# The shared expert's last 64 hidden columns: gate and up in one stationary block, the product across partitions

## The reference, cut to what matters

```python
I_MOE, I_SH = (176, 704)
logits = h @ router_w.T                       # which four experts a token takes
...
g = jnp.einsum('nh,ehi->eni', h, w_gate)      # the routed experts
u = jnp.einsum('nh,ehi->eni', h, w_up)
y = jnp.einsum('eni,eih->enh', jax.nn.silu(g) * u, w_down)
routed = jnp.einsum('enh,ne->nh', y, comb)
shared = jax.nn.silu(h @ sh_gate) * (h @ sh_up) @ sh_down
sg = jax.nn.sigmoid(h @ sh_gate_w)
return (routed + sg * shared).reshape(orig)
```

## Time and profile before

| what | value |
|---|---|
| median of 3 runs | 572.34 us (570.43 to 573.94) |
| the profiled execution | 572.58 us |
| its span, first to last instruction | 570.7 us |
| TensorE busy | 494.5 us of the span |
| mean granted clock of TensorE | 0.951 of full speed |

### The profile page before, as it was taken

The page is one execution under the profiler, slowest core; times in us unless marked ns, Lnnn a source line. Parts: engine busy times, 40 slices in busy tenths (PEclk is TensorE's granted clock), DMA queues, the critical chain, the costliest instruction groups (busy, mean ns, idle before and its releaser), DMA issues.

```text
span 570.7 us, 11095 instructions
## 1 busy us (share of the span) xinstructions
PE 494.5 (87%) x3334; PEld 433.5 (76%) x3338; DVE 446.4 (78%) x1374; ACT 352.7 (62%) x909; POOL 331.7 (58%) x316
## 2 busy tenths in 40 slices
PE   0699989989799998995568999999999999589794
PEld 0477767877698997994358999999999998346582
DVE  4789967966879897855667888989899987859784
ACT  2344547343567675763228887888888889756543
POOL 2547671014368886416698899898777873451300
PEclk9999989999999999996587999999999999959998
DMA  8144454312364656545820000010000000000001
GB/s 279 38 120 138 133 156 121 89 55 65 106 201 113 192 159 202 145 134 148 277 65 29 18 22 28 21 29 1 3 1 2 2 1 2 0 1 0 20 18 38
DMA packets 27960, 45.24 MB, mean 79 GB/s; under 512 B 5696, under 2 KB 18848, under 8 KB 27264
## 3 DMA queue, kind: packets, MB, share of 16 engines
q1 hardware_dynamic: 21056, 28.15, 16.3%
q0 software_dynamic: 3792, 10.74, 7.4%
q10 hardware_dynamic: 3056, 5.65, 3.0%
HBM read 34.63 MB, written 8.85 MB: 76 GB/s over the span
## 4 chain that ended last, share of the span: by engine, by line
PE 49%; DVE 22%; POOL 10%; issue 9%; ACT 5%; DMA 4%; SPq 1%; ACTq 0%; DVEq 0%; POOLq 0%
PE bank L1111 8%; PE bank L432 7%; PE bank L433 7%; PE bank L434 7%; PE bank L1555 5%; POOL yk L629 2%; PE bank L1313 2%; PE bank L1315 2%; PE bank L1314 2%; POOL Q_lo L678 1%; PE bank L1508 1%; DVE X L1676 1%; POOL Q L672 1%; DMA seg<-seg_dram 1%; POOL pr L665 1%
## 5 line engine op out<-in xcount | busy, mean ns | idle before, releaser
L601 POOL DMA_INDIRECT inb<-rows_kept,row_of x47 | 47.1, 1002 | 35.4 <-PE bank L1111 19.3
L984 ACT ACTIVATE pr<-sc,smin 128x256 f32<-128x256 f32 x128 | 63.6, 505 | 0.0
L678 POOL TENSOR_TENSOR Q_lo<-Q,Q_hi 128x512 fp32r<-128x512 f32 x32 | 41.5, 1296 | 15.3 <-ACT Q_hi L729 14.3
L2135 DVE CUSTOM_DVE_ANT_0 sc<-bank,bias 128x256 f32<-128x256 f32 x128 | 46.6, 421 | 0.0
L1624 DVE TENSOR_TENSOR pT_lo<-bank,pT_hi 128x512 fp32r<-128x512 f32 x64 | 41.2, 684 | 6.8 <-ACT pT_hi L729 6.6
L729 ACT ACTIVATE pT_hi<-bank 128x512 fp32r<-128x512 f32 x64 | 35.0, 596 | 15.1 <-PE bank L1111 14.7
L559 POOL TENSOR_TENSOR Wd<-wd_raw,Wd 128x512 fp32r<-128x512 f32 x13 | 16.8, 1293 | 42.2 <-ACT Wd L776 42.2
L672 POOL TENSOR_TENSOR Q<-Q,rot 128x512 f32<-128x512 f32 x32 | 41.1, 1283 | 0.0
L665 POOL TENSOR_TENSOR pr<-pr,srec 128x512 f32<-128x512 f32 x32 | 33.3, 1042 | 13.3 <-DVE srec L2142 13.2
L432 PE MATMUL bank<-K_hi,Q_hi 128*128 128x256 f32 x128 | 37.2, 291 | 4.3 <-POOL Q_lo L678 4.3
L629 POOL DMA_INDIRECT yk<-slots_y,slot x32 | 32.9, 1027 | 10.8 <-issue 5.5
(11 more groups left out here) (351 smaller groups left out, 1954.1 us busy)
## 6 DMA issues: line engine op xcount, KB each, us to landing
slots_y<-yb SPq DMA_DIRECT2D x47, 128.0 KB
wg_raw<-gate_up_dram SPq DMA_DIRECT2D x22, 256.0 KB, 2.6
bw<-bits_dram ACTq DMA_DIRECT2D x3, 1024.0 KB
wd_raw<-down_dram SPq DMA_DIRECT2D x16, 128.0 KB, 2.2
wo<-wo_dram SPq DMA_DIRECT2D x2, 1024.0 KB, 5.7
wd_raw<-down_dram SPq DMA_DIRECT2D x30, 64.0 KB, 2.4
gu_raw<-gate_up_dram SPq DMA_DIRECT2D x6, 256.0 KB, 3.6
X<-x_dram SPq DMA_DIRECT2D x2, 512.0 KB, 6.7
```

Source lines behind the costliest of these rows:

```text
L601: pool.indirect_dma_start(inb[:, j % NIN, :], None, rows_d, bass.IndirectOffsetOnAxis(row_of[:, j:j + 1], 0)).then_inc(slots_in[j % NIN], 16)
L678: pool.tensor_tensor(Q_lo[:, i % 2, :], Q[:, i % 2, :], Q_hi[:, i % 2, :].bitcast(F32), ALU.subtract).then_inc(queries_low_g, 1)
L984: e = act.activation(pr[:, i % 2, z, :], sc[:, i % 2, z, :], ACT.Exp, bias=smin[:, i % 2, z:z + 1], scale=-1.0, accum_out=ssum[:, i % 2, z ...
L2135: dve.tensor_tensor_reduce(sc[:, r, z, :], bank[2 + h][:, u * S:(u + 1) * S], bias[:, TB * b_ + u, :], 1.0, 3.0e38, ALU.add, ALU.min, smin ...
```

## The change

Units 10 and 11 no longer compute with the zeros. The 64 gate columns and the 64 up columns of the last chunk are laid side by side in one block of 128 while the weights are split (gate_and_up reads them from gu_raw, gate_beside_up writes them), so six matmuls give both: the gate on partitions 0 to 63 of one bank, the up on partitions 64 to 127 of the same bank. silu, the product and the splits of hid work on 64 partitions; the product reads gsil from partitions 0 to 63 and the up from partitions 64 to 127. The down matmuls contract over 64 partitions. FULL is 10, the number of units on whole chunks, and HALF_CHUNK is 64. up_p, the count of finished up groups, ends at 10 now, so the last layer's use of that semaphore counts from FULL. No transfer changes; the number of instructions on ScalarE, VectorE, GpSimd and SyncE stays.

```diff
--- before.py
+++ after.py
@@ -410,6 +410,20 @@
         def shared_bank(v, g):
             return (2 * v + g) % 3
 
+        FULL = 2 * (I_SH // P)
+        HALF_CHUNK = I_SH % P
+
+        def rows_of(v):
+            return slice(0, P) if v < FULL else slice(0, HALF_CHUNK)
+
+        def gate_and_up(part, c):
+
+            return part[:, c % 2, :].rearrange("p (g k m) -> p k g m", g=2, k=KD)[:, :, :, 0:HALF_CHUNK]
+
+        def gate_beside_up(part, c):
+
+            return part[:, c % 2, 0:KD * P].rearrange("p (k g m) -> p k g m", g=2, k=KD)
+
         def dn_buffer(e):
 
             return e % 2 if e < NT else 2 if e < EARLY_E else e - EARLY_E
@@ -806,7 +820,11 @@
                 act.wait_ge(gate_up_in[c % 2], 16 * (c // 2 + 1))
                 if c >= 2:
                     act.wait_ge(up_p, 2 * (c - 1))
-                copy(gu_hi[:, c % 2, :], gu_raw[:, c % 2, :]).then_inc(gate_up_high_a, 1)
+                if 2 * c < FULL:
+                    ins = copy(gu_hi[:, c % 2, :], gu_raw[:, c % 2, :])
+                else:
+                    ins = copy(gate_beside_up(gu_hi, c), gate_and_up(gu_raw, c))
+                ins.then_inc(gate_up_high_a, 1)
 
             def hi_dn(c):
                 act.wait_ge(down_in[c % 2], 16 * (c // 2 + 1))
@@ -860,13 +878,15 @@
                 act.wait_ge(gate_p, v + 1)
                 if v >= 2:
                     act.wait_ge(hidden_v, v - 1)
-                act.activation(gsil[:, v % 2, :], bank[shared_bank(v, 0)][:, :], ACT.Silu).then_inc(gate_silu_a, 1)
+                rows = rows_of(v)
+                act.activation(gsil[rows, v % 2, :], bank[shared_bank(v, 0)][rows, :], ACT.Silu).then_inc(gate_silu_a, 1)
 
             def hi_hid(v):
                 act.wait_ge(hidden_v, v + 1)
                 if v >= 2:
                     act.wait_ge(down_p, v - 1)
-                copy(hid_hi[:, v % 2, :], hid[:, v % 2, :]).then_inc(hidden_high_a, 1)
+                rows = rows_of(v)
+                copy(hid_hi[rows, v % 2, :], hid[rows, v % 2, :]).then_inc(hidden_high_a, 1)
 
             def ternary_end(i, c):
                 act.wait_ge(ternary_v, 5 * i + 2 + c)
@@ -1206,7 +1226,7 @@
                     pe.wait_ge(prep_read_v, EARLY)
                     pe.wait_ge(x_after1_v, NE0 * NT)
                 cols = slice(n * HALF, (n + 1) * HALF)
-                for g in range(2):
+                for g in range(2 if v < FULL else 1):
                     if g == 0 and v >= 2:
                         pe.wait_ge(hidden_v, v - 1)
                     if g == 1 and v >= 1:
@@ -1251,8 +1271,9 @@
                     t = n * (NT // 2) + x
                     tile = slice(x * P, (x + 1) * P)
 
-                    e = split3(pe, bank[4 + t // 2][:, (t % 2) * D:(t % 2 + 1) * D], hid_hi[:, v % 2, tile],
-                               hid_lo[:, v % 2, tile], dn_hi[:, c % 2, :], dn_lo[:, c % 2, :],
+                    rows = rows_of(v)
+                    e = split3(pe, bank[4 + t // 2][:, (t % 2) * D:(t % 2 + 1) * D], hid_hi[rows, v % 2, tile],
+                               hid_lo[rows, v % 2, tile], dn_hi[rows, c % 2, :], dn_lo[rows, c % 2, :],
                                c == 0 and t % 2 == 0, c == C_SH - 1, skip_group_check=True)
                 e.then_inc(down_p, 1)
 
@@ -1760,7 +1781,11 @@
 
             def lo_gu(c):
                 dve.wait_ge(gate_up_high_a, c + 1)
-                lo(gu_lo[:, c % 2, :], gu_raw[:, c % 2, :], gu_hi[:, c % 2, :]).then_inc(gate_up_low_v, 1)
+                if 2 * c < FULL:
+                    ins = lo(gu_lo[:, c % 2, :], gu_raw[:, c % 2, :], gu_hi[:, c % 2, :])
+                else:
+                    ins = lo(gate_beside_up(gu_lo, c), gate_and_up(gu_raw, c), gate_beside_up(gu_hi, c))
+                ins.then_inc(gate_up_low_v, 1)
 
             def lo_dn(c):
                 dve.wait_ge(down_high_a, c + 1)
@@ -1918,19 +1943,22 @@
                 dve.tensor_scalar(row_of[:, :], row_f[:, :], N - 1.0, None, ALU.min).then_inc(routing_v, 1)
 
             def hidden(v):
-                dve.wait_ge(up_p, v + 1)
+                if v < FULL:
+                    dve.wait_ge(up_p, v + 1)
                 dve.wait_ge(gate_silu_a, v + 1)
                 if v >= 2:
                     dve.wait_ge(hidden_high_a, v - 1)
                     dve.wait_ge(hidden_low_v, v - 1)
-                dve.tensor_tensor(hid[:, v % 2, :], gsil[:, v % 2, :], bank[shared_bank(v, 1)][:, :], ALU.mult
-                                  ).then_inc(hidden_v, 1)
+                rows = rows_of(v)
+                up = bank[shared_bank(v, 1)][:, :] if v < FULL else bank[shared_bank(v, 0)][HALF_CHUNK:2 * HALF_CHUNK, :]
+                dve.tensor_tensor(hid[rows, v % 2, :], gsil[rows, v % 2, :], up, ALU.mult).then_inc(hidden_v, 1)
 
             def lo_hid(v):
                 dve.wait_ge(hidden_high_a, v + 1)
                 if v >= 2:
                     dve.wait_ge(down_p, v - 1)
-                lo(hid_lo[:, v % 2, :], hid[:, v % 2, :], hid_hi[:, v % 2, :]).then_inc(hidden_low_v, 1)
+                rows = rows_of(v)
+                lo(hid_lo[rows, v % 2, :], hid[rows, v % 2, :], hid_hi[rows, v % 2, :]).then_inc(hidden_low_v, 1)
 
             def late_expert(e):
                 dve.wait_ge(edn_high_a, e + 1)
@@ -2207,7 +2235,7 @@
                                   ALU.mult).then_inc(bit_scaled_v, 1)
 
             def up_b(v):
-                dve.wait_ge(up_p, UNITS + v + 1)
+                dve.wait_ge(up_p, FULL + v + 1)
                 dve.wait_ge(gate_silu_a, UNITS + v + 1)
                 if v >= 2:
                     dve.wait_ge(bit_low_g, v - 1)
```

## The result

The changed kernel took **574.86 us** (median of 20 executions, 572.15 to 576.87) against 572.37 of the kernel before on the same chip (20 executions, 567.19 to 576.38): a ratio of 1.0051 with a 95% interval of 1.0030 to 1.0072. It is slower, by 2.5 us between the medians and 2.9 by the ratio, and outside the range of the forecast.

The account below looks back on a forecast made before the run. It took two register loads, held until hid_lo(9), to bound down(10). A gain of 1.39 us less 0.1 for row changes gave -1.3 us from the median of 572.34: forecast 571.0 us, range 569.0 to 573.3.

Parts of the forecast that it names:

- What bounds down(10): Between down(9) and down(10): two register loads on the matmul engine's sequencer; down(10) starts 3.64 us after they start.
- the room reading: Register loads before down(10): the sequencer can run only 18 matmuls ahead of the array; gain 1.39 us.
- pace: Register loads before down(10): the sequencer needs 0.77 us to hand on down(9)'s 24 instructions; gain 0.74 us.
- a forecast 1.39: Start of down(10): gain in us from the loads starting at 136.6, so down(10) starts at 140.25.
- the idle time: Ahead of down(10): the array would idle 1.95 us instead of 0.74, the sign that the loads are the bound.
- Rival A: At down(10): the sequencer's hand-on time or a later bound limits the gain to 0.7 us, 571.6; chance 0.20.
- Rival B: Units 10 and 11: all the matmul time comes back, 2.75 us, 569.6; chance 0.08.
- The parts: Around units 10 and 11: hidden(10) 0.72 us earlier at unchanged duration, weight splits 0.27 us shorter on VectorE, down(8) hardly delayed.
- Row changes: Into and out of down(10) and down(11): four changes of row count cost 0 to 0.33 us, taken as 0.1.
- Rival D: Units 10 and 11: row changes cost fully and hidden(10) slows by 0.7 or more, no gain, 572.3; chance 0.10.
- the paragraph on 64-row products: At down(10) and down(11): 64 rows of contraction save nothing and cost 0 to 0.33 us in row changes.
- Rival C: Behind 1.95 us idle before down(10): clock falls to half, costing 1.7 us against 1.3 gained, 572.7; chance 0.12.

Follow-up runs that it names:

- kernel 2: Kernel before with down(10) and down(11) contracting over 64 rows only, all else kept; 575.08 us, ratio 1.0010.
- kernel 1: Changed kernel with down(10) and down(11) again over all 128 rows, added rows meeting zero weights; 573.08 us, ratio 0.9976.
- 3: Changed kernel, still 64 rows, with the two register loads moved ahead behind gate_up(7) and gate_up(9); 574.0 us, ratio 0.9983.
- 4: Changed kernel with the register loads moved ahead and down(10) and down(11) over 128 rows; 572.01 us, ratio 0.9967.
- kernel 5: Kernel before with only the two register loads moved ahead, behind gate_up(7) and gate_up(9); 571.26 us, ratio 0.9993.
- kernel 10: Kernel before with gate_up and down of units 2 to 7 over 64 rows; 574.86 us, ratio 1.0041.
- 6: Kernel before with down(10) alone over 64 rows, one execution; 573.91 us.
- 12: Kernel before with down(10) alone over 64 rows, measured again with ten executions; 572.46 us, ratio 0.9993.
- 8: Changed kernel with early register loads and 128 rows in down(10) and down(11), repeated with more executions; 571.52 us, ratio 0.9975.
- 7: Kernel before with down(4) and down(5) over 64 rows, one execution; 573.11 us.
- 11: Kernel before with down(11) alone over 64 rows, down(10) over 128; 571.47 us, ratio 0.9994.

## Why the prediction was wrong

**What bounds down(10): right.** The loads start 0.1 behind hid_lo(9), as down(9) begins; the room reading held and pace (0.77 later) did not. The gain there was 1.29 us against a forecast 1.39, the idle time 2.01 against 1.95. Rival A is out. The Trainium skill ("TensorE: Matmul & The Clock Gate", the table at its head) has the queue of 64 by which it would have been right, and the loads' start here, 0.1 instead of 0.77 behind hid_lo(9) with the same 24 instructions between, speaks against it. Rival B is out for this kernel, for the reason given.

**The parts: right.** hidden(10) on 64 partitions takes 0.69, and starts 2.22 behind gate_up(10) (134.93 - 132.71) where it was 2.95, 0.73 earlier against 0.72. hid_lo(8) no longer waits (0.68 for 1.76); GpSimd's subtraction does instead, 1.85 for 1.29. down(8) starts 1.39 behind gate_up(10), not held up. Row changes: down(10) lasts 142.27 - 140.68 = 1.59, against 143.14 - 141.64 = 1.50, 0.09 for one unit where 0.1 was taken for both; kernel 2's takes 1.58. Rival D is out.

**The step that failed is the paragraph on 64-row products.** It said that they save nothing and cost at most 0.33 us in row changes, and looked no further. The first half holds. It put what these products do to the clock at nothing, without a reason. What the runs showed in its place is that they let the clock fall: with both units over 64 rows the changed kernel ran at 1.0051 of before, with 128 rows at 0.9976. The price of the fall at the first slot down is 21.67 - 19.54 = 2.1 us (changed kernel against 1), 22.88 - 20.64 = 2.2 (2 against before) and 20.26 - 17.85 = 2.4 (3 against 4). In the first pair it does not all stay: kernel 1 has a half-clock stretch of its own from 153.4 on, and at the down of the second slot tile (157.14 and 156.26) 24.43 - 22.87 = 1.6 us of it are left.

**Rival C was the outcome, with the wrong cause, the wrong price and a chance of 0.12.** It priced the fall at 1.7 us, because it counted down(10) and part of down(11); the clock fell only behind down(10), but for 6.8 us, over down(11) and the first products of the slot loop, 2.1 to 2.4 us. It laid the fall to the idle 2 us, and the argument against that held for this place: the earlier trace rows has 1.90 of 3.40 us without a fall, and kernel 1 kept the clock there at 1.88 and at 1.76 of 3.41. It held by little, since 1.84 of 3.42 in the earlier trace rows and 1.72 of 3.41 in kernel 1 did lower it. That is why the chance was low; its 572.7 is 2.2 us under what was measured. Where a change alters two things at one place, the idle time and the kind of products, the rows of before spoke only for one of them.

**Sum after the fact.** In the traces the changed kernel loses 21.67 - 20.64 = 1.0 us up to the first slot down: 1.1 gained by the edit (20.64 - 19.54), 2.1 lost to the clock. The ratio says 2.9 us, with an interval of 1.7 to 4.1. The 0.7 us or more between the two is not accounted for. In this pair of traces the spans differ by 2.2 us, of which 0.3 arose ahead of gate_up(10) (132.71 against 132.38) and 0.8 behind the first slot down; the later stages have half-clock stretches in every kernel, whose length differs from one execution to the next, and whether the change adds to them was not tried.

The Trainium skill ("TensorE: Matmul & The Clock Gate", Part 1: The HAM clock gate) says that the gate follows how busy the engine has been. Taken as share of time this case disagrees: in the array's busy time the changed kernel (2.03 us) stood above kernel 1 (1.88), and it was the one that fell. The same page says (Why this matters for your kernels) that a matmul over few rows takes as long as one over 128; the twelve of down(10), 1.59 us over 64 rows and 1.50 over 128, agree within 0.09, and this is what makes the 64-row form look free.

**The better version.** With 128 rows in the down products and the loads moved ahead, the edit reaches the 2.75 us that rival B named: 20.64 - 17.85 = 2.8 us at the first slot down, of which the loads alone give 0.8 (kernel 5). The two measurements say 0.9967 [0.9935, 0.9999] and 0.9975 [0.9945, 1.0004], 1.9 and 1.4 us less than before: less than the 2.8, and at the edge of what these runs can tell from nothing.

## What to carry to other kernels

Halving the rows of a contraction saved no time on TensorE here (1.59 us against 1.50 for twelve products), and beside idle stretches it cost the clock. A short contraction padded to 128 rows with zero weights was the safer form; where the array was busy without a gap, as between 105 and 119 us of kernel 10, 64 rows did no harm. When a row of before shows idle time that the clock survives, ask with which products it did so. The load of registers that stood between two units waited for the unit ahead of it; ask of such a load whether it can be issued where the array has work queued.

## What the runs showed of the hardware that was not expected

- Products over 64 rows at full pace kept the clock at 1.00 for 13.7 us (kernel 10); with 0.99 us of idle time behind them it fell, where 128-row products with 1.48 us idle did not. What lies behind it, fewer rows or the operands' values, was not separated. The rows that kernel 1 added met weights that are zero and still kept the clock.
- The fall is not the same in each execution: the program of 6 and 12, with 12 of the 24 products of down(10) and down(11) over 64 rows, had it once and once not.
- A load of 24 registers by TensorE's sequencer takes 1.6 to 1.8 us, and what follows two of them came 3.7 us after the first's start, where nothing was queued. Moved up behind gate_up(7) and gate_up(9), they left the array's idle times at those two places at 0.8 to 1.2 us and 0.2 to 0.4 in kernels 3, 4, 5 and 8, which lies among those of the kernels without a load there (0.2 to 1.5 and 0.2 to 0.4).
- hid_lo(8) on VectorE and GpSimd's subtraction start within 0.1 us of each other in these two traces, and one of the two is held up: they took 1.76 and 1.29 us before, 0.68 and 1.85 after, by a change that moved their starts by less than 0.3 us. It is no chance of one trace: the seven profiled kernels before, 2, 5, 6, 7, 11 and 12 have 1.5 to 1.8 and 1.3 us, the six with the changed gate_up 0.68 and 1.8 to 1.9.
